# Filter taps of a long convolution: the transcendental part once for all channels, powers by squaring, both tables on VectorE

## What is computed

```python
dt = jnp.exp(log_dt)
A = A_re + 1j * A_im
C = C_re + 1j * C_im
dtA = dt[:, None] * A
dC = C * (jnp.exp(dtA) - 1.0) / A
powers = jnp.exp(dtA[:, :, None] * jnp.arange(L))
K = 2.0 * jnp.einsum('dn,dnl->dl', dC, powers).real
```

## Time and profile before

| | before |
|---|---|
| median of 3 runs | 5424.76 us (5422.43 to 5425.7) |
| the profiled execution | 5423.54 us |
| its span | 5421.9 us |
| TensorE matmul busy | 4071.0 us, 75% |
| VectorE busy | 2998.4 us, 55% |
| GpSimd busy | 1589.7 us, 29% |
| ScalarE busy | 1368.5 us, 25% |

### The profile page before, as it was taken

The page is one execution under the profiler, slowest core; times in us unless marked ns, Lnnn a source line. Parts: engine busy times, 40 slices in busy tenths (PEclk is TensorE's granted clock), DMA queues, the critical chain, the costliest instruction groups (busy, mean ns, idle before and its releaser), DMA issues. The chain is left out here.

```text
span 5421.9 us, 65111 instructions
## 1 busy us (share of the span) xinstructions
PE 4071.0 (75%) x20932; PEld 3333.7 (61%) x20932; DVE 2998.4 (55%) x9382; ACT 1368.5 (25%) x2058; POOL 1589.7 (29%) x1296
## 2 busy tenths in 40 slices
PE   2341129998578787576877968968799998599998
PEld 2230116776367677466775856756688887488887
DVE  8959952444389899898963545522334343322222
ACT  1120012332355555345541000022211111211111
POOL 2537400000021211112112642400467674233232
PEclk8555559999788888788888989989799999799999
DMA  0016031221601001011003432233312121200000
GB/s 10 18 33 239 35 108 44 80 83 61 190 26 42 27 11 49 15 27 39 13 7 110 145 134 82 97 130 103 124 57 79 60 72 33 90 18 27 19 23 22
DMA packets 238383, 350.33 MB, mean 65 GB/s; under 512 B 67346, under 2 KB 117394, under 8 KB 234258
## 3 DMA queue, kind: packets, MB, share of 16 engines
q1 hardware_dynamic: 145700, 187.77, 11.3%
q10 hardware_dynamic: 89856, 151.04, 8.1%
q0 software_dynamic: 2560, 8.39, 0.4%
HBM read 240.13 MB, written 107.00 MB: 64 GB/s over the span
## 5 line engine op out<-in xcount | busy, mean ns | idle before, releaser
L2747 DVE CAST m_act_hl<-m_g 128x512 fp32r<-128x512 f32 x256 | 139.1, 543 | 896.4 <-ACT m_g L2635 896.4
L1421 PE MATMUL xa_ps_t<-xa_diag,xa_s_buf 128*128 128x128 f32 x4096 | 504.5, 284 | 164.6 <-DVE xa_s_buf L1602 98.4
L1421 PEld LDWEIGHTS xa_ps_t<-xa_diag,xa_s_buf 128*128 128x128 f32 x4096 | 487.3, 198 | 196.1 <-DVE xa_s_buf L1602 117.1
L1550 DVE MAX8 xa_cand<-xa_s_buf 128x8 f32<-128x64 f32 x4096 | 535.4, 217 | 116.4 <-issue 56.8
L2496 POOL TENSOR_TENSOR m_act_hl<-m_g,m_act_hl 128x512 fp32r<-128x512 f32 x256 | 353.6, 1381 | 703.6 <-DVE m_act_hl L2747 703.6
L1366 POOL TENSOR_TENSOR xa_aT<-xa_a,xa_aT 128x512 fp32r<-128x512 f32 x128 | 160.0, 1271 | 1005.5 <-ACT xa_a L1486 1005.5
L2635 ACT ACTIVATE m_g<-m_ps_h,m_b 128x512 f32<-128x512 f32 x256 | 176.2, 688 | 1103.4 <-PE m_ps_h L82 1103.4
L80 PE MATMUL m_ps_h<-m_hT,m_w 128*128 128x512 f32 x1024 | 412.7, 403 | 12.3 <-DVE m_w L2726 7.6
L81 PE MATMUL m_ps_h<-m_hT,m_w 128*128 128x512 f32 x1024 | 404.9, 395 | 0.0
L81 PE MATMUL m_ps_o<-m_w,m_act_hl 128*128 128x512 f32 x1024 | 404.9, 395 | 0.0
L82 PE MATMUL m_ps_h<-m_hT,m_w 128*128 128x512 f32 x1024 | 404.8, 395 | 0.0
(11 more groups left out here) (372 smaller groups left out, 8718.4 us busy)
## 6 DMA issues: line engine op xcount, KB each, us to landing
at_xk<-in_x_dram SPq DMA_DIRECT2D x128, 128.0 KB, 2.7
spectrum<-df_yo ACTq DMA_DIRECT2D x32, 512.0 KB, 2.8
id_raw<-spectrum SPq DMA_DIRECT2D x32, 512.0 KB, 3.7
m_xt<-x ACTq DMA_DIRECT2D x64, 256.0 KB, 3.4
bf_w_dn<-_L_ffn_down_weights_dram SPq DMA_DIRECT2D x7, 2048.0 KB, 7.2
bf_w_up<-in_L_ffn_up_weights_dram ACTq DMA_DIRECT2D x7, 2048.0 KB, 10.1
ky_raw<-in_ctx_dram SPq DMA_DIRECT2D x16, 768.0 KB, 6.2
xa_ks<-kt SPq DMA_DIRECT2D x48, 256.0 KB
```

The lines of the kernel that those rows point to most:

```text
L1421: last = pe.matmul(ps_t[:, c // 4, c % 4, :], s_buf[:, t % 2, h, k0:k0 + P], diag[:, h, :], start=(h == 0 and c % 4 == 0), stop=(h == HEAD ...
L1550: dve.max(out=ranks[h][:, :, g], in_=s_buf[:, t % 2, h, g * SEG:(g + 1) * SEG])
```

## The change

- The parameters, dt and D_skip of all four chunks are loaded at once into wider tiles. The transcendental part runs once, on two powers of exp(dtA) (1 and 32) of all four chunks: 2 x 4 x 64 = 512 columns. `pw` takes these two, and four rounds of squaring fill in powers 2, 4, 8, 16 and 64 to 512. The coefficients are computed once for all chunks, 256 columns wide, after the first `tab[0]`.
- VectorE grows both tables of each chunk one after the other (`first_table`, `second_table`, new `grow`) with one `tmp`. Table 0 of chunk c waits for the copies of table 0 of chunk c - 1, table 1 for all copies of chunk c - 1.
- GpSimd only builds the identity and adds D_skip to tap 0, as soon as `kd` is loaded.
- The turning of chunk c - 1's rows moves behind the taps of chunk c, on TensorE, ScalarE and SyncE. SyncE issues the `tap_rows` store of chunk c, then the eight row stores of chunk c - 1, then the load of `kd` for chunk c. All `Fori` loops are written out.

The diff, cut. In the wide part (L299 to L316) only the tile shapes change; the body of the coefficients (L330 to L349) is the same at the new width.

```diff
-    LEVELS = 10
+    STEPS = 5
...
-        ldt = sb("ldt", [P, 1])
+        ldt = sb("ldt", [P, DC])
         dsk = sb("dsk", [P, DC])
-        par = sb("par", [P, 4, NST])
-        dt = sb("dt", [P, 3])
-        dt_bits = sb("dt_bits", [P, 1], mybir.dt.int32)
-        z = sb("z", [P, 6, LEVELS, NST])
-        z_bits = sb("z_bits", [P, LEVELS, NST], mybir.dt.int32)
-        lam = sb("lam", [P, LEVELS // 2, 2, NST])
-        big = sb("big", [P, 5, 2, NST])
-        w = sb("w", [P, 12, NST])
-        ones = sb("ones", [P, NST])
+        par = sb("par", [P, 4, DC, NST])
+        dt = sb("dt", [P, 3, DC])
+        dt_bits = sb("dt_bits", [P, DC], mybir.dt.int32)
+        z = sb("z", [P, 6, 2, DC, NST])
+        z_bits = sb("z_bits", [P, 2, DC, NST], mybir.dt.int32)
+        pw = sb("pw", [P, STEPS, 2, 2, DC, NST])
+        sq = sb("sq", [P, 2, 2, DC, NST])
+        w = sb("w", [P, 12, DC, NST])
         tab = [sb(f"tab{i}", [P, R, 2, NST]) for i in range(2)]
-        tmp = [sb(f"tmp{i}", [P, 2, R // 2, NST]) for i in range(2)]
+        tmp = sb("tmp", [P, 2, R // 2, NST])
...
-                def load(c):
-                    sp.dma_start(ldt[:, :], rows(A["L0_xattn_log_dt"].rearrange("(n o) -> n o", o=1), c * P, P)).then_inc(s_ld, 16)
-                    for i, name in enumerate(("A_re", "A_im", "C_re", "C_im")):
-                        sp.dma_start(par[:, i, :], rows(A["L0_xattn_" + name], c * P, P)).then_inc(s_ld, 16)
-                def through_dram(c):
-                    sp.wait_ge(s_kc, (P // G) * (c + 1))
+                for v, name in ((ldt, "L0_xattn_log_dt"), (dsk, "L0_xattn_D_skip")):
+                    sp.dma_start(v[:, :], A[name].rearrange("(c p) -> p c", p=P), allow_slow_non_contiguous=True).then_inc(s_ld, 16)
+                for i, name in enumerate(("A_re", "A_im", "C_re", "C_im")):
+                    sp.dma_start(par[:, i, :, :], A["L0_xattn_" + name].rearrange("(c p) n -> p c n", p=P)).then_inc(s_ld, 16)
+                def store(c):
+                    for n in range(NT):
+                        sp.wait_ge(s_oc, NT * c + n + 1)
+                        sp.dma_start(taps_out[n * P:(n + 1) * P, c * P:(c + 1) * P], kT[:, n % 2, :]).then_inc(s_st[n % 2], 16)
+                for c in range(DC):
+                    sp.wait_ge(s_kc, NG * (c + 1))
                     sp.dma_start(rows(tap_rows, c * P, P).rearrange("d (a r) -> a d r", r=R), krow[:, :, :]).then_inc(s_kr, 16)
+                    if c >= 1:
+                        store(c - 1)
                     sp.wait_ge(s_kr, 16 * (c + 1))
                     sp.dma_start(kd[:, :], rows(tap_rows, c * P, P)).then_inc(s_kd, 16)
-                    for n in range(S // P):
-                        sp.wait_ge(s_oc, (S // P) * c + n + 1)
-                        sp.dma_start(taps_out[n * P:(n + 1) * P, bass.ds(c * P, P)], kT[:, n % 2, :]).then_inc(s_st[n % 2], 16)
-                sp.dma_start(dsk[:, :], A["L0_xattn_D_skip"].rearrange("(c p) -> p c", p=P), allow_slow_non_contiguous=True).then_inc(s_dsk, 16)
-                load(0)
-                for c in range(DC):
-                    if c + 1 < DC:
-                        sp.wait_ge(s_pow, c + 1)
-                        load(c + 1)
-                    through_dram(c)
+                store(DC - 1)
...
-                with pool.Fori(0, DC) as c:
-                    pool.wait_ge(s_pow, c + 1)
-                    pool.wait_ge(s_trc, 16 * c)
-                    pool.tensor_tensor(tab[1][:, 0, 0, :], w[:, 10, :], ones[:, :], ALU.mult)
-                    pool.tensor_tensor(tab[1][:, 0, 1, :], w[:, 11, :], ones[:, :], ALU.mult)
-                    pool.drain()
-                    grow(pool, tab[1], tmp[1], big, R)
-                    pool.drain().then_inc(s_tab[1], 1)
+                pool.wait_ge(s_ld, 16 * 6)
+                for c in range(DC):
+                    pool.wait_ge(s_kd, 16 * (c + 1))
+                    pool.tensor_tensor(kd[:, 0:1], kd[:, 0:1], dsk[:, c:c + 1], ALU.add).then_inc(s_skip, 1)
...
+                def turn(c, i):
+                    pe.wait_ge(s_tab[i], c + 1)
+                    for g in range(8):
+                        n = 16 * c + 8 * i + g
+                        if n >= 2:
+                            pe.wait_ge(s_trc, n - 1)
+                        for q in range(4):
+                            last = pe.transpose(ps_t[:, n % 2, q, :], tab[i][:, 4 * g + q, :, :].rearrange("p a n -> p (a n)"), ident[:, :])
+                        last.then_inc(s_tr, 1)
+                def taps(c):
                     pe.wait_ge(s_trc, 16 * (c + 1))
-                    for g in range(P // G):
-                        pe.wait_ge(s_kc, (P // G) * c + (g - 1 if g >= 1 else 0))
+                    for g in range(NG):
+                        n = NG * c + g
+                        if n >= 2:
+                            pe.wait_ge(s_kc, n - 1)
                         for q in range(G):
                             d = g * G + q
-                            last = pe.matmul(ps_k[:, g % 2, q, :], tabT[1][:, :, d], tabT[0][:, :, d], start=True, stop=True)
+                            last = pe.matmul(ps_k[:, n % 2, q, :], tabT[1][:, :, d], tabT[0][:, :, d], start=True, stop=True)
                         last.then_inc(s_k, 1)
+                def rows_turned(c):
                     pe.wait_ge(s_skip, c + 1)
-                    pe.wait_ge(s_kd, 16 * (c + 1))
-                    for n in range(S // P):
-                        pe.wait_ge(s_oc, (S // P) * c + (n - 1 if n >= 1 else 0))
+                    for n in range(NT):
+                        if NT * c + n >= 2:
+                            pe.wait_ge(s_oc, NT * c + n - 1)
                         pe.transpose(ps_o[:, n % 2, 0:P], kd[:, n * P:(n + 1) * P], ident[:, :]).then_inc(s_o, 1)
+                for c in range(DC):
+                    turn(c, 0)
+                    turn(c, 1)
+                    taps(c)
+                    if c >= 1:
+                        rows_turned(c - 1)
+                rows_turned(DC - 1)
...
+                def rows_copied(c):
+                    for n in range(NT):
+                        act.wait_ge(s_o, NT * c + n + 1)
+                        if NT * c + n >= 2:
+                            act.wait_ge(s_st[n % 2], 16 * ((NT // 2) * c + n // 2))
+                        act.activation(kT[:, n % 2, :], ps_o[:, n % 2, 0:P], ACT.Copy).then_inc(s_oc, 1)
+                for c in range(DC):
                     for n in range(16):
                         act.wait_ge(s_tr, 16 * c + n + 1)
+                        if n == 0 and c >= 1:
+                            act.wait_ge(s_k, NG * c)
                         i, g = n // 8, n % 8
                         act.activation(tabT[i][:, 4 * g:4 * g + 4, :], ps_t[:, n % 2, :, :], ACT.Copy).then_inc(s_trc, 1)
+                    if c >= 1:
+                        act.wait_ge(s_kr, 16 * c)
+                    for g in range(NG):
+                        act.wait_ge(s_k, NG * c + g + 1)
                         act.activation(krow[:, g * G:(g + 1) * G, :], ps_k[:, g % 2, :, :], ACT.Copy).then_inc(s_kc, 1)
+                    if c >= 1:
+                        rows_copied(c - 1)
+                rows_copied(DC - 1)
...
+                def grow(table, c, which):
+                    for k in range(STEPS):
+                        m = 2 ** k
+                        re, im = table[:, 0:m, 0, :], table[:, 0:m, 1, :]
+                        pr = pw[:, k, which, 0:1, c, :].broadcast_to([P, m, NST])
+                        pi = pw[:, k, which, 1:2, c, :].broadcast_to([P, m, NST])
+                        for part, (x, y, op) in enumerate(((pr, pi, ALU.subtract), (pi, pr, ALU.add))):
+                            dve.tensor_tensor(tmp[:, 0, 0:m, :], re, x, ALU.mult)
+                            dve.tensor_tensor(tmp[:, 1, 0:m, :], im, y, ALU.mult)
+                            dve.drain()
+                            dve.tensor_tensor(table[:, m:2 * m, part, :], tmp[:, 0, 0:m, :], tmp[:, 1, 0:m, :], op)
+                            dve.drain()
+                dve.wait_ge(s_ld, 16 * 6)
+                W = [w[:, i, :, :] for i in range(12)]
+                dve.tensor_copy(dt[:, 1, :], ldt[:, :])
+                dve.drain()
+                exp(dt[:, 1, :], dt[:, 2, :], dt_bits[:, :], dt[:, 0, :])
                 for c in range(DC):
+                    for i, a in enumerate((are, aim)):
+                        dve.tensor_scalar(z[:, i, 0, c, :], a[:, c, :], dt[:, 0, c:c + 1], None, ALU.mult)
...
+                dve.tensor_scalar(z[:, 0:2, 1, :, :], z[:, 0:2, 0, :, :], float(R), None, ALU.mult)
...
+                dve.tensor_tensor(pw[:, 0, :, 0, :, :], X, CO, ALU.mult)
+                dve.tensor_tensor(pw[:, 0, 0, 1, :, :], X[:, 0], SI[:, 0], ALU.mult)
+                dve.scalar_tensor_tensor(out=pw[:, 0, 1, 1, :, :], in0=X[:, 1], scalar=-1.0, in1=SI[:, 1],
```

(71 more changed lines are left out.)

87 lines of the change are left out of this document (32 added, 55 removed).

## The result

5305.47 us against 5423.60 us of the kernel before on the same chip (medians of 4 runs each): ratio 0.9783 [0.9770, 0.9796]. The profiled execution has a span of 5305.2 us. That is 118 us less where 132 were forecast, and 0.5 us outside the upper end of the range.

A forecast was written before the change was run, and what follows sets the result against it. VectorE's table work was taken to bound the taps stage, TensorE after the change. Stage end 402.1 to 270.2 us is 132 us less: profiled execution 5423.5 becomes 5291.5, median 5292.7, stated as 5292; range 5279 to 5305.

The forecast's parts named there:

- The failed step: Whole kernel: stages follow one another behind a barrier, so the 132 us saved in the taps stage shorten the end equally.
- The unrolled loops remove branches ... nothing: Taps stage: removed branches and three ScalarE table reloads all lie under idle time now, so they gain nothing.
- Rival D: Taps stage: late unrolled instructions or a longer two-queue wait add 3 us per TensorE period, about 5302; chance 0.08.
- D: Taps stage: new wait of the first row stores behind the 512 KB tap-row store, 3.0 us a round, bounds 0 to 4.5.
- the second turn of chunk 1: Taps stage, TensorE: after waiting for table 1 at 136.0 us, turning it takes 6.0 us, taps from 142.3.
- VectorE's part: Taps stage: transcendental part starts at 6.4 us, table 0 at 52.2, coefficients at 70.4, table 1 ready at 99.6.
- Rival A: Taps stage: VectorE's tables stay at 34 us without GpSimd, end 5408; chance 0.05 for anything from 5310 to 5412.
- period of 42.3 us: Taps stage, TensorE per chunk: turns 13.0, taps 18.7, rows 7.2, row-store wait 3.0, handovers 0.4 us.
- rival B: Taps stage: no row-store wait, or 16 turn groups in about 11 us; at most 15 us more gain, 5277; chance 0.12.
- The sum: Taps stage ends at 270.2 instead of 402.1 us, 132 us less, giving a kernel time of 5292 us.

The follow-up runs named there:

- act_store: Kernel after, with TensorE's stream padded, and the row stores issued from ScalarE's queue instead of SyncE's: 5297.41 us, ratio 0.9763.
- pool_table: Kernel after, padded, with table 1 grown on GpSimd again, transcendental part still done once and coefficients ahead of both tables: 5324.40 us, ratio 0.9803.
- a_pad72: Kernel after with 144 already met waits (72 instructions) added on TensorE ahead of the taps stage: 5297.38 us, ratio 0.9761.
- rows_early: Kernel after, padded, with chunk c - 1's rows turned and stored before the taps of chunk c, for c = 1 and 2: 5284.53 us, ratio 0.9738.
- a_pad176: Kernel after with 352 already met waits (176 instructions) added on TensorE ahead of the taps stage: 5321.96 us, ratio 0.9803.

## Why the prediction was wrong where it was

- **The failed step**: "whatever the taps stage loses, the end loses, if the later stages keep their own times (the change touches none of them)". The second MLP did not keep its time: +12.1 us, of which the padding gives back 10.5 and so shows them to be the place of its loop in TensorE's stream. The rest of the sum alone would have given about 5293 us. "The unrolled loops remove branches ... nothing" is the same mistake from the other side: unrolling also adds instructions ahead of every later loop. Rival D had named late instruction streams, but inside the taps stage and at 3 us a period, where the trace shows none.
- **Mis-sized, D**: 3.0 forecast, the difference of two landings; 4.7 measured in the mean and over the stated bound of 4.5 in two of three rounds, with a store ahead that landed in 5.7 us and not 4.5. Why the same store is slower in this kernel, even alone, was not found. That a store behind the tap rows waits them out held on one queue (5.7 us) and not across two (2.6 us in act_store).
- **Mis-sized, the second turn of chunk 1**: 7.6 us from the table's end to the taps (136.18 to 143.78), 6.0 forecast. With D of the last round, which no turn covers (row stores to 258.85, forecast 255.8), this makes 273.4 out of 270.2.
- **VectorE's part was right**: start 6.2 (6.4), table 0 at 52.4 (52.2), coefficients at 70.5 (70.4), table 1 ready at 99.8 (99.6) and of chunk 1 at 136.2 (136.0). Products of 1024 and 512 elements take the time of the butterfly stage's. Rival A is out; chunk 0 of pool_table shows the other engine as the reason for 3.2 us.
- **TensorE became the bound, as forecast, but its period of 42.3 us is right by luck**: two errors cancel. From the last row store to the taps are 10.6 and 11.1 us (174.78 to 185.37, 217.28 to 228.35) where 13.0 and a handover were forecast, because TensorE starts the next turns while ScalarE still copies rows; that is half of rival B, which had them in about 11. Against it stands the longer D. VectorE waited for ScalarE only once, 7.5 us, not 5 us in each chunk.
- **What gave the gain**: everything but the engine of table 1 (the transcendental part done once, the new order) 102 us, 402.1 to 299.7, not split further by a run; both tables on VectorE 28.6 more behind it, mostly because GpSimd's 40 us table no longer stands between two turns, but only 12.7 alone.
- **The sum**: +3.2 us in the taps stage, +12.1 in the second MLP, -0.1 in all others together are the 15.3 us between the forecast span (5289.9) and 5305.2. Within that -0.1, +5.0 us in the butterfly and attention stages (953 to 961 us over all kernels run) stay unexplained. Of these 4.2 lie in the windowed attention, which has two levels: 566.3 to 567.5 us in six kernels, a_pad72 and rows_early among them, and 570.9 to 571.9 in the kernel after, a_pad176, pool_table and act_store. It is not the same cause: q8 moved 20 packets in that stage in all ten kernels.

## What to carry to other kernels

Writing a loop out, or adding code ahead of it, moves every later hardware loop in that engine's stream: compare the lengths of the untouched stages, look for a stop without a releaser at their backward branches, and count the packets of the instruction queue in both kernels, before explaining them otherwise. A long loop like this one is worth placing; here 144 empty waits gave 10.5 us of span. A small store that a copy waits for is worth issuing ahead of a big one or in its own time, since another queue did not help here. Before work is shared between two engines, time the slower one's part to its end: here it, and not the first engine's slowdown, set the period.

## What was not expected of the hardware

- A backward branch over 1665 TensorE instructions stopped it for at most 0.7 us when the loop touched 7 pieces of 256 instructions and for up to 4.4 us (3.74 in the row shown) when it touched 8; the loop in 7 pieces was passed twice without one instruction packet. Behind the two long stops of the kernel after the granted clock fell to 0.50, which cost 2.4 and 1.6 us.
- The same 512 KB store in 128-byte pieces, alone on the queues, moved at about 215 GB/s in one kernel and 135 in the other. The cause is open.
- 460 extra waits on a semaphore already reached, ahead of the first matmul, did not show in the time (0.9997 [0.9988, 1.0007]).
